# Linear attention beside a mixture of experts: the first loads by quarters of the contraction, a new order of the first casts, norms and products, output weights split slice by slice, small tables moved

## The reference

```python
xn = _layernorm(x, axis=-1)
# attention: 16 heads of 32
qkv = xn @ W_qkv + b_qkv                        # [.., 3 * 512]
q_prime, k_prime = relu(q), relu(k)             # times cos and sin of the position
kv_cos = einsum('bhld,bhle->bhde', k_cos, v)    # and kv_sin
context = einsum('bhld,bhde->bhle', q_cos, kv_cos) + einsum('bhld,bhde->bhle', q_sin, kv_sin)
output = context / (norm[..., None] + EPS)      # norm: q with the sums of k
attn = output @ W_out + b_out
# experts: 8, each takes the 1024 tokens of a batch that want it most
probs = softmax(einsum('bsd,ed->bse', xn, choice_w))
G, I = top_k(swapaxes(probs, -1, -2), 1024)
h = silu(einsum('bekd,edf->bekf', x_in, w1))    # x_in: the chosen rows, f = 1024
out = zeros.at[b_idx, I].add(G[..., None] * einsum('bekf,efd->bekd', h, w2))
return x + attn + out
```

## Time and profile before

| | |
|---|---|
| runs of the kernel before | 2490.52, 2497.65, 2500.50 us |
| median | 2497.65 us |
| profiled execution | 2497.8 us |
| its span | 2495.9 us |
| PE busy | 2396.7 us (96%) |
| PEld busy | 2013.4 us (81%) |
| DVE busy | 1345.1 us (54%) |
| POOL busy | 1077.1 us (43%) |
| ACT busy | 831.3 us (33%) |

### The profile page before, as it was taken

The page is one execution under the profiler, slowest core; times in us unless marked ns, Lnnn a source line. Parts: engine busy times, 40 slices in busy tenths (PEclk is TensorE's granted clock), DMA queues, the critical chain, the costliest instruction groups (busy, mean ns, idle before and its releaser), DMA issues.

```text
span 2495.9 us, 34661 instructions
## 1 busy us (share of the span) xinstructions
PE 2396.7 (96%) x12544; PEld 2013.4 (81%) x12544; DVE 1345.1 (54%) x2654; ACT 831.3 (33%) x1458; POOL 1077.1 (43%) x959
## 2 busy tenths in 40 slices
PE   8999999999999999999998998999999998999898
PEld 7889988898999887777776786787786787787677
DVE  7777776687777786334335245245245245245331
ACT  4445544454454553122223223223223223223111
POOL 0100034200002565565665565566565565566441
PEclk9999999999999999999999999999999999999999
DMA  7555334355544446224224223324324323322122
GB/s 198 160 126 142 105 58 73 56 152 151 129 123 80 60 79 142 44 41 113 49 43 107 49 48 81 69 50 108 54 48 94 58 51 77 73 49 45 35 39 30
DMA packets 125947, 205.38 MB, mean 82 GB/s; under 512 B 28264, under 2 KB 53480, under 8 KB 125552
## 3 DMA queue, kind: packets, MB, share of 16 engines
q0 software_dynamic: 57088, 118.02, 26.5%
q1 hardware_dynamic: 68720, 85.42, 11.6%
HBM read 119.22 MB, written 100.93 MB: 88 GB/s over the span
## 4 chain that ended last, share of the span: by engine, by line
PE 89%; issue 4%; DVE 4%; another core or an unknown queue 1%; ACT 1%; DMA 1%; POOL 0%; POOLq 0%; DVEq 0%; SPq 0%; ACTq 0%
PE ps L1351 29%; PE ps L1353 28%; PE ps L1352 28%; PE ps L1444 2%; PE ps L1581 1%; DVE h_lo L1318 1%; PE ps L1378 1%; DVE one_lo L906 1%; DVE h_hi L1316 0%; DMA xo<-in_L_attn_x_dram 0%; DMA normed_rows<-xo 0%; DVE w_lo L1322 0%; DVE stats L810 0%; DVE qT L1034 0%
## 5 line engine op out<-in xcount | busy, mean ns | idle before, releaser
L462 POOL DMA_INDIRECT rows<-normed_rows,idx_row x512 | 540.1, 1055 | 156.1 <-issue 156.1
L1351 PE MATMUL ps<-w_hi,h_hi 128*128 128x512 f32 x1024 | 414.2, 404 | 43.4 <-issue 29.9
L570 POOL DMA_INDIRECT out_dram<-y,idx x128 | 227.9, 1780 | 477.1 <-ACT y L792 473.7
L1351 PE MATMUL ps<-xi_hi,w_hi 128*128 128x512 f32 x1024 | 406.7, 397 | 8.7 <-issue 8.6
L1352 PE MATMUL ps<-w_lo,h_hi 128*128 128x512 f32 x1024 | 408.3, 399 | 5.3 <-issue 5.2
L1353 PE MATMUL ps<-w_hi,h_lo 128*128 128x512 f32 x1024 | 407.9, 398 | 2.8 <-issue 2.6
L1316 DVE CAST h_hi<-hf 128x512 fp32r<-128x512 f32 x256 | 111.2, 435 | 546.5 <-issue 289.8
L1352 PE MATMUL ps<-xi_lo,w_hi 128*128 128x512 f32 x1024 | 401.9, 392 | 0.0
L1353 PE MATMUL ps<-xi_hi,w_lo 128*128 128x512 f32 x1024 | 400.3, 391 | 0.8 <-issue 0.7
L772 ACT ACTIVATE hf<-ps 128x512 f32<-128x512 f32 x256 | 153.0, 598 | 666.3 <-PE ps L1353 448.2
L1351 PEld LDWEIGHTS ps<-w_hi,h_hi 128*128 128x128 f32 x1024 | 198.1, 193 | 92.4 <-issue 42.4
(11 more groups left out here) (176 smaller groups left out, 4117.9 us busy)
## 6 DMA issues: line engine op xcount, KB each, us to landing
xo<-in_L_attn_x_dram SPq DMA_DIRECT2D x32, 512.0 KB, 4.7
normed_rows<-xo SPq DMA_DIRECT2D x32, 512.0 KB, 4.5
out_dram<-bo POOLq DMA_DIRECT2D x16, 1024.0 KB, 9.1
out_dram<-xo POOLq DMA_DIRECT2D x64, 256.0 KB, 4.0
w_raw<-in_L_ffn_w_dram SPq DMA_DIRECT2D x32, 512.0 KB
w_raw<-in_L_ffn_w_dram SPq DMA_DIRECT2D x8, 2048.0 KB
xn<-normed_rows SPq DMA_DIRECT2D x96, 128.0 KB, 2.4
rows<-normed_rows,idx_row POOLq DMA_INDIRECT x512
```

Source lines behind the costliest of these rows:

```text
L462: nc.gpsimd.indirect_dma_start(rows[:, tt, a, :], None, pieces[:, :], bass.IndirectOffsetOnAxis(ap=idx_row[:, b, tile, a:a + 1], axis=0)). ...
L570: nc.gpsimd.indirect_dma_start(of[:, :], bass.IndirectOffsetOnAxis(ap=idx[:, u * TPB + tt:u * TPB + tt + 1], axis=0), y[:, tt, :], None, c ...
L1351: nc.tensor.matmul(dst, a_hi, b_hi, start=start, stop=False, skip_group_check=True)
```

## The change

**Loads.** A weight load's four transfers now each fill all 128 partitions with a quarter of the contraction (`k`), where each filled 32 partitions with all of it. SP's order is now x, identity, router weights, query weights, query bias, value weights, key weights, constants, key bias, value bias. The query bias has a semaphore of its own (`bq_in`).

**First block.** DVE makes the low part of the first quarter of the query weights between the norms of the first block's two halves. PE turns two tiles, the router weights, and then makes the first half of the first query part before it turns the other two tiles; the second query part is made in halves too. The turned tiles stand in other PSUM banks. ACT casts the value weights one query output later than before. For batch 0, `norm_half(1, 0)` moves from ahead of the first block's loop into it, behind `k_low` of the first tile, and ACT's `sqrt(1, 0)` with it. The waits for the constants and biases move behind.

**Output weights.** `out_weights` handles one slice at a time, each behind `k_low` of one tile (`k_ready`), in blocks 1 and 2.

**Small tables.** They are made in steps 18 and 20 of stage 2 of batch 0. The waits for `bits_in` and `iota_ready` move to `search_start`.

The diff, cut to its core (new names for the semaphores, the constants `CON_LOADS = 2` and `X_BANKS = (0, 1, 2, 7)`, and moved waits at the two ends are left out):

```diff
...
-                    sp.dma_start(raw_weights(part)[i * HD:(i + 1) * HD, :, :],
-                                 w_qkv[i * P:(i + 1) * P, part * D:(part + 1) * D].rearrange("(k j) d -> j k d", j=HD)
+                for k in range(KD):
+                    sp.dma_start(raw_weights(part)[:, k, :],
+                                 w_qkv[:, part * D:(part + 1) * D].rearrange("(i k j) d -> k i j d", i=HPG, k=KD)[k]
                                  ).then_inc(w_in[part], 16)
...
             sp.dma_start(ch_rows, choice_w[:, :]).then_inc(ch_in, 16)
             load_weights(Q)
+            with nc.allow_non_contiguous_dma("small transposed load"):
+                sp.dma_start(bq[:, :], b_qkv[0:D].rearrange("(m p) -> p m", p=P)).then_inc(bq_in, 16)
+            load_weights(V)
+            load_weights(K)
             sp.dma_start(con[:, C_BLOCK:C_END], consts[:, C_BLOCK:C_END]).then_inc(table_in, 16)
-            load_weights(V)
-            with nc.allow_non_contiguous_dma("small transposed load"):
-                sp.dma_start(bq[:, :], b_qkv[0:D].rearrange("(m p) -> p m", p=P)).then_inc(con_in, 16)
+            sp.dma_start(bk[:, :], b_qkv[D:2 * D].rearrange("(a d) -> a d", a=1).to_broadcast([P, D])).then_inc(con_in, 16)
             sp.dma_start(bv[:, :, 0:P], b_qkv[2 * D:3 * D].rearrange("(a g c) -> a g c", a=1, g=G).to_broadcast([P, G, P])
                          ).then_inc(con_in, 16)
-            sp.dma_start(bk[:, :], b_qkv[D:2 * D].rearrange("(a d) -> a d", a=1).to_broadcast([P, D])).then_inc(con_in, 16)
-            load_weights(K)
...
+            def out_weights(c, k):
+
+                if c == 1:
+                    pool.wait_ge(w_in[O], 16)
+                    nc.gpsimd.tensor_copy(wo_hi[:, k, :], raw_weights(O)[:, k, :]).then_inc(wo_hi_ready, 1)
+                else:
+                    pool.wait_ge(wo_hi_ready, k + 1)
+                    nc.gpsimd.tensor_tensor(wo_lo[:, k, :], raw_weights(O)[:, k, :], wo_hi[:, k, :].bitcast(F32),
+                                            ALU.subtract).then_inc(wo_ready, 1)
...
+                    for t in range(TPB):
+                        if t % 2 == 0:
+                            pool.wait_ge(k_read, AHEAD + (b * NBLK + c) * TPB + t + 1)
+                            if t == 0:
+                                base_copy(c)
+                            else:
+                                base_bias(c)
+                        if b == 0 and c in (1, 2):
+                            pool.wait_ge(k_ready, c * TPB + t + 1)
+                            out_weights(c, t)
+                    if b == 0 and c == 2:
+                        pool.wait_ge(wo_ready, KD)
+                        pool.sem_inc(wo_free, NBLK // 2)
...
             q_weights(0)
-            turned_hi(0, 0, None, 4)
-            turned_hi(0, 1, None, 5)
+            turned_hi(0, 0, None, X_BANKS[0])
+            sqrt(0, 1)
+            turned_hi(0, 1, None, X_BANKS[1])
...
             q_weights(1)
-            turned_hi(0, 2, None, 6)
-            turned_hi(0, 3, None, 7)
+            turned_hi(0, 2, None, X_BANKS[2])
+            turned_hi(0, 3, None, X_BANKS[3])
             q_weights(2)
             q_weights(3)
...
-            kv_weights(V)
-            act.wait_ge(con_in, CON_LOADS * 16)
+            act.wait_ge(bq_in, 16)
...
                     q_out(n, 0, 0, 5, 1)
+                    if n == 0:
+                        kv_weights(V)
                     q_out(n, 0, 1, 6, 2)
                     if n == 0:
                         kv_weights(K)
+                        act.wait_ge(table_in, 16)
                     q_out(n, 0, 2, 5, 3)
                     q_out(n, 0, 3, 4, 4)
-                    sqrt(n + 1, 0)
+                    if n > 0:
+                        sqrt(n + 1, 0)
...
                         k_high(n, t)
+                        if n == 0 and t == 0:
+                            sqrt(n + 1, 0)
...
+            norm_half(0, 0, 0, False)
             q_weights(0)
-            turned_lo(0, 0, 4)
-            turned_lo(0, 1, 5)
+            norm_stats(0, 1)
+            turned_lo(0, 0, X_BANKS[0])
+            turned_lo(0, 1, X_BANKS[1])
+            norm_rows(0, 1, 0, False)
...
             q_weights(1)
-            turned_lo(0, 2, 6)
-            turned_lo(0, 3, 7)
+            turned_lo(0, 2, X_BANKS[2])
+            turned_lo(0, 3, X_BANKS[3])
             q_weights(2)
+            q_weights(3)
             norm_store(0)
-            q_weights(3)
             norm_store(1)
...
-                norm_half(n_first + 1, 0, 2 * b + 1, False)
+                if b > 0:
+                    norm_half(n_first + 1, 0, 2 * b + 1, False)
                 for t in range(TPB):
                     if t == TPB - 1:
                         turned_lo(n_first + 1, t - 1)
@@ -1061,13 +1072,13 @@
                         turned_lo(n_first + 1, t if t == TPB - 1 else t - 1)
                     k_low(n_first, t)
                     if t == 0:
+                        if b == 0:
+                            norm_half(n_first + 1, 0, 2 * b + 1, False)
                         norm_stats(n_first + 1, 1)
...
                         norm_store(t - 1)
                 for trig in range(2):
                     k_sum(n_first, TPB - 1, TPB - 1, trig)
-                if b == 0:
-                    small_tables()
...
+                    if b == 0 and t in (18, 20):
+                        small_tables(t // 2 - 9)
...
+            for t in range(2):
+                turn_x(0, t, X_BANKS[t])
+            pe.wait_ge(ch_perm_ready, 1)
+            for k in range(KD):
+                last = nc.tensor.transpose(ch[:, k, :], ch_perm[:, k * P:(k + 1) * P], ident[0:E, 0:E])
+            last.then_inc(ch_turned, 1)
             pe.wait_ge(w_ready, 1)
             pe.wait_ge(xT_ready, 2)
...
                 q_half(0, 5, 0)
+                if b == 0:
+                    for t in range(2, TPB):
+                        turn_x(0, t, X_BANKS[t])
+                    pe.wait_ge(w_ready, 2)
+                    q_half(1, 6, 0)
...
                     q_half(0, 5, 1)
-                    if first:
+                    if not first:
+                        kv(n - 1, TPB - 1)
+                    pe.wait_ge(lg_read, AHEAD + n * TPB)
+                    if first and b == 0:
+                        q_half(1, 6, 1)
                         pe.wait_ge(w_ready, KD)
                     else:
-                        kv(n - 1, TPB - 1)
-                    pe.wait_ge(lg_read, AHEAD + n * TPB)
-                    q_rest(1, 6)
+                        q_rest(1, 6)
                     pe.wait_ge(q_read, AHEAD + n * KD + 1)
                     q_rest(2, 5)
```

71 lines of the change are left out of this document (24 added, 47 removed).

## The result

The changed kernel takes 2519.1 us (median of 15 runs, 2507.79 to 2532.34), the kernel before beside it 2500.78 (15 runs, 2490.15 to 2521.33). The ratio is 1.0056, with a 95% interval of 1.0035 to 1.0077: slower by a little over half a per cent, some 14 us, where 2.25 us had been forecast. The two medians stand 18.3 us apart, near the upper end of that interval. The profiled execution took 2518.33 us, its span is 2516.5, 20.6 longer than before.

What follows compares the result with a forecast made beforehand. PE, busy 96% of the span, was taken to bound the kernel. Terms of +0.8, +3.7, -0.5 and -1.75 sum to +2.25 us on the median 2497.65, giving 2499.9, rounded to 2500; range 2491 to 2508.

Steps and rivals of the forecast that it cites:

- The loads: Query weights' load: at 128 partitions a transfer it runs at 376 GB/s, landing 1.9 us earlier, at 10.3.
- These landings release nothing of PE's: Value and key weights, landing about 14 and 17 us, are needed only after later query parts, so PE gains nothing.
- Term 1: Start up to the third query part: first product 0.9 us earlier, but transposes and a later clock rise; +0.8 us.
- Term 2: First block: the moved norm enters DVE's busy chain with only 0.3 us cover, so PE waits; +3.7 us.
- Rival (a): First block's moved norm is hidden by room in DVE's chain, making its cost 0: 2496 us; chance 22%.
- Term 3: Block 1's third query part: small tables leaving DVE there end PE's wait, and stage 2 hides them; -0.5 us.
- Term 4: Block 2: output weights by slices end PE's wait (-2.10), with half of 0.7 paid at the fourth slice; -1.75 us.
- (b): Loads: quarters no faster because rows are strided; query weights land at 12.1, start costs +2.5, 2502 us; chance 12%.
- (c): Start: PE's clock stays low until 21 us, costing +1.25 us more, 2501 us; chance 10%.
- (d): From block 2 on: DVE's lateness is handed on, 13 blocks pay 1 us each, 2513 us; chance 3%.

Runs made afterwards that it cites:

- The pair with equal first products: The change without quarters and moved norm, its query weights early over two queues (2379.52 us, 1.0002 of the kernel before), beside early halves (2376.07 us, 0.9989).
- early halves: Kernel before with sliced output weights, tables in stage 2, and half the query weights issued early on ACT's queue: 2376.07 us, ratio 0.9989.
- the blocks of 32 rows: Kernel before with only the query weights loaded by quarters, each quarter in four transfers of 32 partitions: 2611.88 us, ratio 1.0000.

## Why the prediction was wrong

Forecast: 2500, from 2491 to 2508, 3% for slower by more than 0.5%. Measured: 1.0056. By its steps:

**The loads: this step failed.** I compared 376 with 220 and 210 GB/s, found that the slow ones had 32 partitions a transfer, and gave 128 partitions the speed of x. Partitions are not all that differs between x and the quarters. x, the old loads and w1 all have an outermost dimension of 32 or more; the quarters have 4, and no row that I used had so few. I took "128 partitions" for the shape and didn't read the pattern in the diff, `"(i k j) d -> k i j d"`, as the chip gets it: 4 by 32 by 512. The landing came at 18.81 (the first cast, which it frees), 8.5 us after my figure and 6.7 after the old one, beyond both bounds (9.8 and 12.1). The Trainium skill has the rule, in "DMA: Bandwidth & Descriptors", section "Why a DMA increments its semaphore by 16 and not by 1": a transfer is spread over the largest number of engines up to 16 that divides the slowest dimension longer than one on both sides. This case agrees: 96 to 102 GB/s and 26.2% with 4, 49 GB/s and 13.1% with 2. With that rule the estimate would have been 4 of 16 engines at x's 376 GB/s, 94 GB/s, 11.2 us for the query weights instead of 2.8. By the working of the prediction that lands them at 18.7.

**"These landings release nothing of PE's" failed with it.** At 100 GB/s, 3.1 MB take 31 us, and the key weights land at 40.88. Then the cover that I named is gone, two query parts of 2.8 us, and PE waits 5.71 us and loses 1.8 more to the clock.

**Term 1, the start: wrong in its input, right in its first steps, and one queue forgotten.** From the first cast to the first product I had 4.6 us; 4.67 or 4.68 were measured in five kernels with the new order. From there to the first product of values the change was to cost 1.7 more than before (0.8 for the whole start, with the product 0.9 earlier); in the changed kernel it is 1.96 without the wait. So with a landing at 18.81 this step gives a first product at 23.4, where 23.49 was found. What it left out is that the old order, with loads as late, is quicker from cast to product (2.7 us). The pair with equal first products shows what I had not costed: it differs by 3.4. The clock rose 5.4 us after the first product there (4.4, 5.8 and 6.0 in the other three kernels with the new order and landings of 12.8 to 14.3), and the eight transposes were paid at the low clock. But the clock's first rise wanders between kernels with the same work (last section), so this part of the pair's difference can't be charged to the order from one trace each; the medians, 3.45 and 3.9 us for the new order, say that the whole is real. And I had followed the order on PE, DVE and ACT, but not on SP: the store of the first normed rows moves behind `q_weights(3)`, the load of block 1's x stands behind it, and DVE waited 2.31 us for it. In the changed kernel the moved norm hides this last part. With the landing of 11.00, 0.7 after my figure, the first product of values came 2.25 us later than before. So with my landing term 1 would have been about 1.6 up to there, an estimate from these rows, and not +0.8.

**Term 2, the moved norm: right.** Forecast +3.7, in four waits of 0.8, 0.7, 0.1 and 2.1; in the changed kernel three places have 0.9, 0.4 and 2.2, and PE takes 3.5 us longer over them (39.21 to 51.35 before, 56.36 to 72.01 now). That block 0's logits to block 1's also take 3.51 longer is chance: there 0.6 of half clock comes in and the tables' 0.6 goes. Putting the norm back gave 3.43 (median), of which the rows put 1.5 down to half clock and 2.2 to the norm, less than 3.5 because x of block 1 is late for a norm in the old place and the clock rose later in that trace. Rival (a), a norm that is hidden, is refuted.

**Term 3, the tables: right.** -0.5 forecast; the row that waited is gone, and in the changed kernel the stretch behind the waits is 0.60 shorter, with slices and tables on the kernel before 0.4 to 0.6.

**Term 4, the slices: right in its mechanism.** Forecast -1.75, of it 0.35 paid for the fourth slice; by rows it is -1.5, of it 0.6 for that slice (38.17 instead of 37.59). The forecast took 3.49 against 0.69 us for the reach of POOL, and the second of these rows reads PSUM, the first doesn't; but an xT_lo of the same kind as the first takes 0.68 us at 120.87, without POOL beside it, so the comparison holds.

By PE's last product ahead of block 1's first turned tile the sum is: 13.2 for the quarters (56.36 less 43.15 with the loads as before), 3.9 for the new order (43.15 less 39.21), 3.5 for the norm, -0.6 for the tables, -1.5 for the slices. That is 18.5; block 3 shows 18.56.

**The rivals.** (b) said "quarters are no faster" and gave it 2.5 us. It had the right place, but its end was the old speed; I had no rival in which the quarters are slower than what they replace. (c), a late rise of the clock, came in three experiments (5.4 to 6.0 us after the first product, where it asked for some 6) but not in the changed kernel. (d) did not come: the first logits of blocks 1, 2, 3 and 4 are 37.59, 38.17 and 37.57 us apart. The range was too narrow for the same reason: the bound of an unknown cost was taken from the rows that lay nearest in kind (other weights), while the new pattern lay outside all rows.

**A version that beats both.** Slices alone, or slices and tables, stand at 0.9989 (0.998 to 0.9998 for the slices, and for slices, tables and early halves): about 0.1% better than the kernel before. The tables' 0.4 to 0.6 us show in rows only. Nothing else of the change gained.

## What to carry to other kernels

When a load's pattern is changed, write down the dimensions of both sides as they go to the DMA, slowest first, and compare the outermost with that of every transfer from whose speed you argue; a queue whose share of the 16 engines stays near 4/16 or 2/16 while transfers wait tells the rest. A new order must be costed on the issuing engine too: a store that moves takes with it the load that stands behind it. And when all rows of a kind have a property in common that the new operation lacks, their spread is no bound for it.

## What the runs showed of the hardware

- A transfer with an outermost dimension of 4 uses four DMA engines (26.2% of 16, 102 GB/s), with one of 2 two (13.1%, 49 GB/s): 25 GB/s each. Rows that are pieces of 2 KB out of 6 KB don't slow it: x, in whole rows over all engines, has 376/16 = 23.5 GB/s each.
- The clock can fall again after a wait of 2 us, and need not. With the loads as before and the norm moved, PE waited 2.02 us before 58.42, and some 1.2 us later the clock was at its lower level (1.2 GHz) for 3.3 us, which cost 1.5. The changed kernel waited 2.04 us at the same place and kept the upper one. With the norm back (a wait of 0.84) nothing fell. Stretches of PE in the first and in the changed kernel (start and end, us, busy and number of products, granted clock, share of DMA, GB/s):

```profile
56.40:58.40 2.00, 0.00 (x0) 1.00 0.34 28
60.50:62.50 2.00, 2.00 (x6) 0.50 1.09 142
...
73.70:75.70 2.00, 2.00 (x14) 1.00 0.99 139
```

  The same holds for PE's wait of 1.75 us in block 2: with the quarters alone and with the blocks of 32 rows the clock fell behind it (to 0.50 for 3.4 us, and the block took 1.5 and 1.8 us longer), in three other traces it did not. I had charged a wait with its own length; it can cost about twice that, and one trace doesn't tell which.
- The first rise of the clock wanders: 1.7, 4.3, 2.3 and 4.1 us after the first product in four kernels whose work up to there is the same (the kernel before, slices, early halves, slices and tables). One trace gives no price for it to better than a microsecond.
- A second queue raised the rate (308 GB/s with two), but what it gave the query weights depended on what else was sent. In the old order the first cast came at 16.84 and 12.26, against 12.14 to 12.74 with one queue; in the new order, with constants and biases last, at 11.00, against 12.84 to 14.26. That SP's later loads took the share is my reading of the rows; it was not tested by itself.
